# A four-stage graph and expert network on one core: double result buffers in the expert networks, a one-comparison round in a radix search

## The reference, cut to what matters

```
x = x + segment_sum(edge_weight * layernorm(x)[src], dst)               # stage 1: messages
x = x + moe(layernorm(x))          # stage 2: 8 experts, top 2 of each row, D=256, H=1024, exact gelu
x = x + layer_norm(gcn(relu(gcn(layernorm(x), W1, b1)), W2, b2))        # stage 3: two graph convolutions
x = x + capacity_ffn(layernorm(x))                                      # stage 4
```

## Time and profile before

| | us |
|---|---|
| median of 3 runs | 5736.0 (5732.77 to 5741.24) |
| the profiled execution's own time | 5697.18 |
| its span on the core | 5695.2 |
| PE busy | 3772.3 (66%) |
| POOL busy | 2840.8 (50%) |
| DVE busy | 2176.9 (38%) |
| ACT busy | 1946.3 (34%) |

### The profile page before, as it was taken

The page is one execution under the profiler, slowest core; times in us unless marked ns, Lnnn a source line. Parts: engine busy times, 40 slices in busy tenths (PEclk is TensorE's granted clock), DMA queues, the critical chain, the costliest instruction groups (busy, mean ns, idle before and its releaser), DMA issues.

```text
span 5695.2 us, 62339 instructions
## 1 busy us (share of the span) xinstructions
PE 3772.3 (66%) x13751; PEld 2767.5 (49%) x13751; DVE 2176.9 (38%) x6102; ACT 1946.3 (34%) x4712; POOL 2840.8 (50%) x2838
## 2 busy tenths in 40 slices
PE   4555557777698799999355555555655555555568
PEld 2333335555587688888233333333433333333457
DVE  7433345556465411111233333333533333333731
ACT  6333332222355322222333333333433333333521
POOL 2666665556400133333466666666266666666013
PEclk6776778999897999999666676676867676766779
DMA  3333336666696244444433333333233333333212
GB/s 103 103 108 105 108 112 187 199 197 207 193 302 228 91 111 111 111 111 102 141 92 92 94 91 92 91 94 90 83 92 92 91 92 92 91 93 90 80 43 32
DMA packets 322625, 660.17 MB, mean 116 GB/s; under 512 B 60683, under 2 KB 142923, under 8 KB 322150
## 3 DMA queue, kind: packets, MB, share of 16 engines
q0 software_dynamic: 148960, 365.25, 22.2%
q1 hardware_dynamic: 173318, 290.95, 16.9%
HBM read 488.94 MB, written 174.87 MB: 117 GB/s over the span
## 4 chain that ended last, share of the span: by engine, by line
PE 22%; issue 13%; another core or an unknown queue 7%; DVE 6%; ACT 2%; DVEq 1%; DMA 1%; SPq 1%; POOL 0%; POOLq 0%; ACTq 0%
PE bank L1931 17%; DVE reg_b L1448 3%; PE bank L1878 2%; PE bank L1889 1%; PE bank L1850 1%; DVEq L327 1%; ACT reg_a L843 1%; DVE small L914 1%; ACT reg_a L853 1%; DMA conv_rows<-work 0%; DVEq L1448 0%; PE bank L1912 0%; SPq L576 0%; PE bank L1840 0%
## 5 line engine op out<-in xcount | busy, mean ns | idle before, releaser
L1931 PE MATMUL bank<-work,reg_a 128*128 x3520 | 1327.4, 525 | 1154.4 <-issue 858.5
L694 POOL DMA_INDIRECT work<-conv_rows,tables x1662 | 1575.9, 948 | 937.5 <-issue 473.1
L1931 PEld LDWEIGHTS bank<-work,reg_a 128*128 128x128 f32 x3520 | 832.7, 258 | 1649.0 <-issue 1529.6
L1448 DVE TENSOR_TENSOR reg_b<-reg_b,bank 128x257 f32 x1760 | 743.7, 423 | 1648.1 <-PE bank L1931 636.3
L655 POOL DMA_INDIRECT messages<-work,small x880 | 886.8, 1008 | 567.9 <-issue 242.9
L1789 PE MATMUL bank<-reg_b,reg_a 128*128 x1760 | 607.2, 479 | 487.4 <-issue 267.3
L853 ACT ACTIVATE reg_a<-reg_a,ones 128x512 f32<-128x512 f32 x440 | 316.1, 718 | 1486.0 <-remote 744.1
L764 ACT ACTIVATE work<-bank,tables 128x256 f32<-128x256 f32 x880 | 399.9, 474 | 1012.7 <-PE bank L1789 608.2
L1789 PEld LDWEIGHTS bank<-reg_b,reg_a 128*128 128x128 f32 x1760 | 359.8, 229 | 703.0 <-issue 667.4
L843 ACT ACTIVATE reg_a<-iota,tables 128x128 f32<-128x128 f32 x1760 | 562.6, 391 | 41.8 <-DVEq L1585 13.1
L676 POOL DMA_INDIRECT residual_rows<-work,slot_t x112 | 178.2, 1591 | 478.1 <-DVE work L1406 306.8
(11 more groups left out here) (382 smaller groups left out, 3812.9 us busy)
## 6 DMA issues: line engine op xcount, KB each, us to landing
reg_b<-messages SPq DMA_DIRECT2D x290, 258.0 KB
reg_a<-in_L_ffn_W_dram SPq DMA_DIRECT2D x56, 1024.0 KB, 5.4
work<-messages SPq DMA_DIRECT2D x128, 258.0 KB, 3.5
reg_a<-item_rows SPq DMA_DIRECT2D x110, 256.0 KB
work<-conv_rows,tables POOLq DMA_INDIRECT x1662
b_rows<-messages SPq DMA_DIRECT2D x96, 258.0 KB
messages<-work,small POOLq DMA_INDIRECT x880
conv_rows<-work SPq DMA_DIRECT2D x14, 896.0 KB, 4.0
```

Of the source, the lines that this page charges most:

```text
L694: g.indirect_dma_start(GC[:, u, 0:D], None, table, bass.IndirectOffsetOnAxis(ap=BSRC[:, b_:b_ + 1], axis=0)).then_inc(z(f"conv_in{u // 4}" ...
L1448: v.tensor_tensor(acc, acc, ps[i % 8][:, 0:D + 1], ALU.add).then_inc(z("conv_add"), 1)
L1931: pe.matmul(ps[i % 8][:, 0:D + 1], OHP[:, i % OHR, :], GCf[:, bass.ds(offs[i % 4], D + 1)], start=True, stop=True).then_inc(z(f"{tag}_mm"), 1)
```

## The change

- `YO` gets two buffers of two halves each. `result` works half by half: it waits for its half's product, adds the bias (128x256), multiplies by the gate, and waits only for the scatter of the same half of pair j-2.
- Product 2 writes each half to a bank of its own, in turn over banks 5, 6 and 7, and signals each half; it waits for the bank's reader three halves back.
- `scatter`: h=0 waits for both scatters of pair j-1, h=1 for no other scatter. Empty slots of odd tiles get another 128 spare rows (N + 128 + partition), and `residual_rows` grows by 128 rows, which SP fills as well.
- The search: the candidate bits of every round stand in a table, made in the second convolution pass as 11 more steps of side work, with a twelfth for `SOME` = VAL - 1; the scores of the padding are set to -1 once before the search; in a round one OR makes the candidates, one comparison of 7 x 49 columns the hits, and one reduction the counts.

```diff
@@ -96,7 +97,7 @@
     FLAST = KSEL - (NF - 1) * P
-    FPAD = T * P + P
+    FPAD = T * P + 2 * P
...
@@ -253,11 +254,11 @@
-        HTB, GX, XE, YO, HS = carve(0, HC * PP, 2 * D, KC * PP, 2 * D, D)
+        HTB, GX, XE, YO, HS = carve(0, HC * PP, 2 * D, KC * PP, 4 * D, D)
...
         XE = XE.rearrange("p (c n) -> p c n", c=KC)
-        YO = YO.rearrange("p (h d) -> p h d", h=2)
+        YO = YO.rearrange("p (b h d) -> p b h d", b=2, h=2)
...
@@ -297,11 +298,13 @@
         WV = sm(T)
+        HITS = EQ[:, 0:7 * T].rearrange("p (k t) -> p k t", t=T)
...
         CNTS = sm(7)
+        BITS, SOME = CNT[:, 0:77].bitcast(I32).rearrange("p (r k) -> p r k", k=7), START1[:, 0:T]
...
@@ -533,7 +536,7 @@
-            sp.dma_start(x2_t[T * P:FPAD, :], X[:, 0, :]).then_inc(z("x1_out"), 16)
+            sp.dma_start(x2_t[T * P:FPAD, :].rearrange("(k p) d -> p k d", p=P), X[:, 0:2, :]).then_inc(z("x1_out"), 16)
...
@@ -671,11 +674,12 @@
                         pool.wait_ge(z("net_out"), 2 * (j + before) + h + 1)
-                        if j or h:
-                            pool.wait_ge(z(f"net_added{1 - h}"), 16 * (j + before + h))
+                        if j and h == 0:
+                            for k in range(2):
+                                pool.wait_ge(z(f"net_added{k}"), 16 * (j + before))
...
                             ap=sidx_t[:, 2 * j + h:2 * j + h + 1], axis=0),
-                            YO[:, h, :], None, compute_op=ALU.add).then_inc(z(f"net_added{h}"), 16)
+                            YO[:, j % 2, h, :], None, compute_op=ALU.add).then_inc(z(f"net_added{h}"), 16)
...
@@ -703,7 +707,7 @@
                 pool.wait_ge(z(f"net_added{k}"), 16 * (NT // 2))
-            pool.wait_ge(z("net_mm2"), NT // 2)
+            pool.wait_ge(z("net_mm2"), NT)
...
@@ -796,7 +800,7 @@
                     if j >= 2:
-                        act.wait_ge(z("net_mm2"), j - 1 + before)
+                        act.wait_ge(z("net_mm2"), 2 * (j - 1 + before))
...
@@ -1361,7 +1365,11 @@
                 step(v.tensor_copy(gidx_t[:, 0:tiles], r))
-                step(v.tensor_scalar(free, ps[2][:, 0:tiles], 0.0, SC[:, 0:1], ALU.is_equal, ALU.mult))
+                for h in range(2):
+                    ins = v.tensor_scalar(free.rearrange("p (j h) -> p j h", h=2)[:, :, h],
+                                          ps[2][:, 0:tiles].rearrange("p (j h) -> p j h", h=2)[:, :, h],
+                                          0.0, SC[:, h:h + 1], ALU.is_equal, ALU.mult)
+                step(ins)
...
@@ -1394,17 +1402,16 @@
-                    v.wait_ge(z("net_mm2"), j + 1 + before)
-                    if j:
-                        for h in range(2):
-                            v.wait_ge(z(f"net_added{h}"), 16 * (j + before))
                     b_ = B2B[:, bass.ds(e * D, D)] if experts else FB2B
-                    v.tensor_tensor(YO, ps[5 + j % 2][:, :].rearrange("p (h d) -> p h d", h=2), per_column(b_, 2),
-                                    ALU.add).then_inc(z("net_y"), 1)
-                    v.wait_ge(z("net_y"), j + 1 + before)
                     for h in range(2):
-                        v.tensor_scalar(YO[:, h, :], YO[:, h, :], gate_t[:, 2 * j + h:2 * j + h + 1], None, ALU.mult
-                                        ).then_inc(z("net_out"), 1)
+                        n = 2 * (j + before) + h
+                        v.wait_ge(z("net_mm2"), n + 1)
+                        if j >= 2:
+                            v.wait_ge(z(f"net_added{h}"), 16 * (j - 1 + before))
+                        v.tensor_tensor(YO[:, j % 2, h, :], ps[5 + n % 3][:, 0:D], b_, ALU.add).then_inc(z("net_y"), 1)
+                        v.wait_ge(z("net_y"), n + 1)
+                        v.tensor_scalar(YO[:, j % 2, h, :], YO[:, j % 2, h, :], gate_t[:, 2 * j + h:2 * j + h + 1], None,
+                                        ALU.mult).then_inc(z("net_out"), 1)
...
@@ -1435,6 +1442,16 @@
+            def search_parts():
+
+                for r, (low, bits) in enumerate(SEARCH):
+                    for k in range((1 << bits) - 1):
+                        ins = v.tensor_scalar(BITS[:, r, k:k + 1], ZEROC.bitcast(I32), (k + 1) << low, None, ALU.bitwise_or)
+                    step(ins)
+                    yield
+                step(v.tensor_scalar(SOME, VAL, 1.0, None, ALU.subtract))
+                yield
+
...
@@ -1488,6 +1505,7 @@
             v.memset(VAL, 1.0)
+            v.tensor_scalar(SC[:, 1:2], PCOL, float(N + P + 1), None, ALU.add)
...
@@ -1583,7 +1601,7 @@
             v.engine_nop().then_inc(z("conv_ready"), 1)
-            item_sums("p2", score_parts())
+            item_sums("p2", itertools.chain(score_parts(), search_parts()))
...
@@ -1641,19 +1659,16 @@
             step(v.tensor_scalar(SIGN, SIGN, 2.0, -1.0, ALU.mult, ALU.add))
-            step(v.tensor_scalar(RM, WV, SIGN, None, ALU.mult))
+            step(v.scalar_tensor_tensor(RM, WV, SIGN, VAL, ALU.mult, ALU.mult))
+            step(v.tensor_tensor(RM, RM, SOME, ALU.add))
             step(v.memset(THR, 0.0))
-            for low, bits in SEARCH:
+            for r, (low, bits) in enumerate(SEARCH):
                 n = (1 << bits) - 1
-                for k in range(n):
-                    ins = v.tensor_scalar(CAND[:, k:k + 1].bitcast(I32), THR.bitcast(I32), (k + 1) << low, None,
-                                          ALU.bitwise_or)
-                step(ins)
-                for k in range(n):
-                    ins = v.scalar_tensor_tensor(EQ[:, T * k:T * k + T], RM, CAND[:, k:k + 1], VAL, ALU.is_ge,
-                                                 ALU.mult, accum_out=CNTS[:, k:k + 1])
-                total = counted(ins, n)
+                step(v.tensor_tensor(CAND[:, 0:n].bitcast(I32), BITS[:, r, 0:n], THR.bitcast(I32).to_broadcast([P, n]),
+                                     ALU.bitwise_or))
+                step(v.tensor_tensor(HITS[:, 0:n, :], per_column(RM, n), in_columns(CAND[:, 0:n], T), ALU.is_ge))
+                total = counted(v.tensor_reduce(CNTS[:, 0:n], HITS[:, 0:n, :], AX.X, ALU.add), n)
...
@@ -1881,14 +1896,15 @@
                     pe.wait_ge(z("net_gelu"), (j + 1 + before) * HC)
-                    if j >= 2:
-                        pe.wait_ge(z("net_y"), j - 1 + before)
                     for h in range(2):
+                        n = 2 * (j + before) + h
+                        if n >= 3:
+                            pe.wait_ge(z("net_y"), n - 2)
...
                             w_ = w2ff[:, bass.ds(e * (HC * D) + k * D, D)] if experts else fw2s[:, k, :]
-                            ins = pe.matmul(ps[5 + j % 2][:, h * D:(h + 1) * D], HT[j % 2][:, k, h * P:(h + 1) * P], w_,
+                            ins = pe.matmul(ps[5 + n % 3][:, 0:D], HT[j % 2][:, k, h * P:(h + 1) * P], w_,
                                             start=(k == 0), stop=(k == HC - 1))
-                    ins.then_inc(z("net_mm2"), 1)
+                        ins.then_inc(z("net_mm2"), 1)
...
```

More of the change, by code:

```diff
@@ L10 @@
+import itertools
 from contextlib import ExitStack
```

## The result

The changed kernel takes **5704.6 us** (median of 6 runs, 5697.27 to 5708.82) where the kernel before takes 5736.97 in the same measurement (6 runs, 5721.64 to 5748.01). The ratio is 0.9947, with an interval from 0.9933 to 0.9961. The sum forecast 23.4 us less, a ratio of 0.9959, and 5712.6 us. The sum's ratio lies inside the interval, near its upper end, and the time inside the range of 5703 to 5728 us, 8 us under the forecast and less than 2 above the lower end.

What follows compares the result with a forecast made beforehand. PE was taken to bound the networks, POOL's gathers the convolution passes, and chains the network ends and search. Terms 9.4 + 7.7 + 6.6 - 0.3 = 23.4 us took the 5736.0 us median to 5712.6, range 5703 to 5728.

Steps and rivals of the forecast that it cites:

- PE is the bound inside the networks: Both networks: PE is busy nearly throughout, so the change gains nothing inside the 69 pairs.
- The rival of stalls at the half-wise signals: Networks: PE stalls at the per-half signals, 0.34 us per pair cancels the gain, 5736 us; chance 0.07.
- The end of the expert network: After PE's last product there: the last scatter goes at once, 9.4 us earlier, and all that follows with it.
- The end of the last network: After the last product of the program: last scatter at 5678.85 in place of 5686.58, 7.7 us earlier.
- The search: Ten search rounds on DVE and PE: 0.71 us less each, net 6.6 us after the last round and masking.
- The side work: Second convolution pass: the table's added DVE steps cost 0; without cover they cost 6.6 us.
- a rival at 6.6 us: Second convolution pass: DVE's small instructions hold up POOL and each step is paid, 5719.2 us; chance 0.05.
- The slots: Instruction making the spare rows, twice in the program: one becomes two, taken as 0.3 us more.
- The lower end of the range: 5703 us: the search's 343 columns cost half, gaining 4 us more, and a run lies 5 us low.
- a pass that left 1210 us by over 5: Convolution passes: a pass length leaving 1210 us by more than 5 was named as a sign of being wrong.
- tables moved in DRAM: Convolution passes: moved tables slow gather landings and lengthen POOL's ring waits; 0.3 us per wait gives 5752 us; chance 0.04.
- the serial rival: Ends of both networks: scatters still queue at 4.53 us, gaining 6.1 and 4.5 us, 5719.1 us; chance 0.06.

## Why the prediction was right, point by point

**PE is the bound inside the networks: right.** The expert network's matmuls take 803.5 us before and after, in all kernels between 808.9 and 809.8 us from first gather to last product. Neither halved signals, nor three banks, nor one buffer, nor a serial queue changed that. The rival of stalls at the half-wise signals is out: PE is idle for 2.6 us of 803.5, as before.

**The end of the expert network: 9.4 forecast, 9.0 measured** (10.24 less 1.25 us behind the last product; 14.1 less 5.06 at SP's loads). What the step missed is POOL's start: it put 0.02 us between gate and scatter (0.87 us behind the product in all, "within 1 us"), and the scatter started 2726.67 - 2726.26 = 0.41 us behind the gate's end. The 0.02 was read off a row that groups two instructions. The line `2718.57 0.62 DVE L1406 ... x2` of the kernel before ends at 2719.19 and POOL's scatter starts at 2719.21, but the 0.62 us are two gates, and the scatter waits for the first of them alone, which is over 0.35 us after 2718.57: the start took 0.29 us there too. Behind the last scatters it was 0.41 and, in the last network, 0.28. The first half of the last pair did wait for a landing and did fit in front, as worked out.

**The end of the last network: 7.7 forecast, 7.5 measured** (8.60 less 1.13), by the same miss.

**The search: 6.6 forecast, 6.6 to 6.7 measured**, round by round and part by part. The row that decided was the spacing of the removed instructions, and not their durations. By the rule that the prediction took from the Trainium skill (VectorE: DVE Perf Modes, "The DRAIN you can't avoid") the search would have gained 22 us. By that the search alone, on the 5128 us chip, would have had a ratio of 0.9957; it had 0.9984 (0.9975 to 0.9994). The same section also says that a next operation which is not held starts earlier, and that is what the trace has: seven one-column instructions of 0.15 us fill 0.52. So the rounds of before ran unchained neighbours over each other, and the new ones had only that shortened time to gain from.

**The side work: free, as taken.** In every kernel, with the table of bits, without it and with four times as much of it, the second pass is within 3.0 us of the first (the widest: 1044.6 and 1047.6 us in the kernel with serial scatters). The rule of the Trainium skill (SBUF — State Buffer, "SBUF: two separate sides") that a DVE operation in a two-port mode locks GpSimd out of writing descriptors was a rival at 6.6 us; no run here shows such a lock, since POOL's 788 us of busy time stayed the same under 395 more DVE instructions, 284 of them one-column ones of the table.

**The scatters do not queue behind each other: right.** They stand 1.85 us apart where both are ready, and a landing takes 3.8.

**The slots: 0.3 forecast, 0.25 measured.**

The terms measured in the traces are 9.0 + 7.5 + 6.6 - 0.25 = 22.9 us. The medians moved by 32.4, 28.1 and, in two parts, by 16.5 + 8.9 = 25.4 and 18.6 + 9.8 = 28.4 us. All are somewhat above 22.9, and the sum's ratio is inside all intervals. Whether a few microseconds more are gained somewhere isn't shown: the mechanism and the terms were right, but the 9 us by which the first medians moved further than the sum are not accounted for by them. The lower end of the range, near which the time came out, stood for a cheaper comparison and reduction, and these cost what was forecast.

**What went against the text: a pass that left 1210 us by over 5.** That was named as a sign of being wrong, and the profile had it, 11 us in each pass. The rival behind it, tables moved in DRAM, did not show on the two quick chips: the networks' edits changed the four passes by +0.5, +0.7, -4.1 and -2.3 us, and a gather's median time to landing is 2.7 us there in the kernel before and with the moved tables alike. But POOL never waits for the ring on these chips, so their passes could not have shown a slightly slower ring. On the slower chips five profiles of changed kernels have passes of 1218.8 to 1221.4 us and two of the kernel before 1209.5 to 1211.7, and on no chip are profiles of both known to have been taken. The timed runs speak for the chip: 22 us of longer passes would have left 1 us of the gain, and the five ratios on those chips are 0.9947 to 0.9965. There is also a sum for the 5727 us chip. Its message stage (first to last of the 880 scatters of messages), which no edit touches, lasts 1412 us in four profiles (1397.7 to 1422.5), 28 us more than the 1383.8 of the chip with 5684 us. Put into the latter's profile of 5677.1 us that gives 5705, and the kernel before takes 5727 there: 20 us are missing, which is what passes of 1220 would add. The other way speaks that pass and message stage do not go together from profile to profile: the first profile of the kernel before has 1407.8 us of messages and passes of 1210, the changed kernel's second one 1397.7 and 1221. So that the longer passes belong to the chip is argued and not shown; a profile of the kernel before on such a chip would settle it.

## What to carry to other kernels

Where an engine is the bound for 800 us, 160 us of waits behind it are worth only what of them lies behind its last instruction; read the last two items of the pipeline there, with instructions that a row groups taken apart. Break the longest link first and measure the rest against it: here unchained scatters gave most, halves the remainder, and a second buffer nothing beside these two. Cost a row of unchained DVE instructions by the distance of its first to its last start, and never compare two profiled spans without comparing a stretch that the change leaves alone.

## What the runs showed that was not expected

**Chips differ by 12% on this kernel, and it is in the two convolution passes and the message stage.** From the 5128 us chip to the one of the first profile, the first pass grows from 1045 to 1210 us and the message stage from 1169 to 1408, while the expert network is 809 us on both. In the pass every engine is busy for the same time. POOL's gathers follow at 1.25 us on both, and 831 of them make 1040 us, which is the quick chip's pass: POOL never waits for the ring there. On the other chips it stops some 60 times a pass for 2.5 to 2.9 us. The mean granted clock, which moves between 2.4 and 1.2 GHz in these passes, is 0.77 of the full one on the quick chip and 0.68 on the other, where PE does its matmuls in small groups with waits between (at 3201.51 us of the first profile two matmuls stand behind 4.3 us of idle time); in the expert network, with PE busy throughout, it is 1.00. PE's busy time in the pass is the same (670 and 664 us), so slower matmuls alone aren't the 165 us. Which comes first, the lower clock or the stops of the ring, the runs don't tell.

**Two scatters that wait for each other cost more than a landing.** In 54 of the 56 pairs of the kernel before the second scatter starts 4.39 to 5.11 us after the first (4.53 in the pair of the earlier trace rows); in one pair in the middle it is 5.92, and in the last pair it was 5.85 before (2728.99 to 2734.84) and 5.61 with halves. Unchained they stand 1.85 us apart. The forecast had put 4.53 everywhere; so the serial rival's gain at the end of the expert network was put at 6.1 us and was 5.1 (10.24 less 5.14). The landing itself is not what grows (it takes 3.8 us in the pair of the earlier trace rows, in the middle one and in the last). POOL's next scatter follows 0.73 to 0.87 us behind it, but 2.10 in that middle pair and 2.01 in the last one, the same on the quick chip. What POOL does in these 2 us the profile doesn't show.
